# Stores of pairwise products from one DMA queue or from two: odd chunks issued from GpSimd, even chunks from SP

## The reference

```
_I, _J = np.triu_indices(NUM_FEAT, k=1)
proj = jnp.einsum('bnd,ed->bne', x, W)
out = proj[:, PAIR_I, :] * proj[:, PAIR_J, :]
```

## Time and profile before

| | |
|---|---|
| median of three runs | 511.1 us (510.85 to 511.14) |
| span of the profiled execution | 508.2 us |
| VectorE busy | 437.3 us, 86% |
| TensorE busy (matmul) | 71.3 us, 14% |
| ScalarE busy | 54.3 us, 11% |
| GpSimd busy | 0.7 us |
| bytes moved by DMA | 215.10 MB, 423 GB/s over the span |

### The profile page before, as it was taken

The page is one execution under the profiler, slowest core; times in us unless marked ns, Lnnn a source line. Parts: engine busy times, 40 slices in busy tenths (PEclk is TensorE's granted clock), DMA queues, the critical chain, the costliest instruction groups (busy, mean ns, idle before and its releaser), DMA issues.

```text
span 508.2 us, 2204 instructions
## 1 busy us (share of the span) xinstructions
PE 71.3 (14%) x481; PEld 65.4 (13%) x481; DVE 437.3 (86%) x220; ACT 54.3 (11%) x162; POOL 0.7 (0%) x6
## 2 busy tenths in 40 slices
PE   6965100000930000000660000000000000000000
PEld 5854100000920000000660000000000000000000
DVE  3999988888999999899999999999899989999900
ACT  5752000000720000000450000000000000000000
POOL 0000000000000000000000000000000000000000
PEclk9995555555875555555695555555555555555555
DMA  8999999999999999999999999999999999999996
GB/s 311 411 423 433 427 431 428 430 431 434 428 431 432 434 431 432 431 429 434 434 430 432 431 434 432 431 432 432 429 434 431 427 427 427 429 429 431 431 431 277
DMA packets 17430, 215.10 MB, mean 423 GB/s; under 512 B 1936, under 2 KB 2064, under 8 KB 7184
## 3 DMA queue, kind: packets, MB, share of 16 engines
q1 hardware_dynamic: 14400, 209.72, 96.7%
q10 hardware_dynamic: 3024, 5.31, 2.8%
HBM read 10.55 MB, written 204.47 MB: 423 GB/s over the span
## 4 chain that ended last, share of the span: by engine, by line
DMA 68%; DVE 21%; issue 5%; PE 1%; DVEq 0%; SPq 0%; ACT 0%; ACTq 0%
DMA out_dram<-products 67%; DVE products L248 21%; DMA w_in<-in_L_rec_W_dram 1%; PE proj_ps L182 0%; PE turned_ps L172 0%; SPq L145 0%; DVEq L248 0%; PE w_ps L162 0%; ACT proj L217 0%; ACT x_turned L206 0%; DVEq L271 0%; ACT w_turned L201 0%; SPq L144 0%; DVEq L247 0%; ACTq L205 0%
## 5 line engine op out<-in xcount | busy, mean ns | idle before, releaser
L248 DVE TENSOR_TENSOR products<-proj 128x384 f32 (+36 forms) x220 | 437.3, 2045 | 46.3 <-DMA out_dram<-products 37.3
L182 PE MATMUL proj_ps<-w_turned,x_turned 128*128 128x128 f32 x320 | 60.5, 319 | 181.5 <-ACT x_turned L206 181.3
L182 PEld LDWEIGHTS proj_ps<-w_turned,x_turned 128*128 128x128 f32 x320 | 48.9, 219 | 186.3 <-ACT x_turned L206 184.4
L206 ACT COPY x_turned<-turned_ps 128x256 f32<-128x256 f32 x80 | 30.0, 379 | 174.0 <-DVEq L257 171.9
L172 PE MATMUL turned_ps<-identity,x_in 128*128 128x128 f32 x160 | 34.4, 306 | 5.7 <-ACT proj L217 5.1
L217 ACT COPY proj<-proj_ps 128x256 f32<-128x256 f32 x80 | 29.7, 373 | 31.4 <-issue 19.0
L172 PEld LDWEIGHTS turned_ps<-identity,x_in 128*128 128x128 f32 x160 | 23.1, 161 | 6.6 <-issue 5.3
L201 ACT ACT_TABLE_LOAD x1 | 1.3, 1283 | 1.2 <-PEq L284 1.2
L162 PE MATMUL w_ps<-identity,w_in 128*128 128x128 f32 x1 | 0.4, 447 | 4.1 <-DMA w_in<-in_L_rec_W_dram 4.1
L162 PEld LDWEIGHTS w_ps<-identity,w_in 128*128 128x128 f32 x1 | 0.2, 182 | 4.0 <-issue 4.0
L201 ACT COPY w_turned<-w_ps 128x128 f32<-128x128 f32 x1 | 0.3, 265 | 2.1 <-PE w_ps L162 2.1
## 6 DMA issues: line engine op xcount, KB each, us to landing
out_dram<-products SPq DMA_DIRECT2D x80, 2496.0 KB, 24.0
x_in<-in_r_x_dram SPq DMA_DIRECT2D x20, 256.0 KB, 6.1
x_in<-in_r_x_dram ACTq DMA_DIRECT2D x20, 256.0 KB, 29.8
w_in<-in_L_rec_W_dram ACTq DMA_DIRECT2D x1, 64.0 KB, 3.2
```

The lines of the kernel that those rows point to most:

```text
L182: last = pe.matmul(proj_ps[group % 2][:, k, :], x_turned[group % 2][:, k, :], w_turned[:, :], start=True, stop=True)
L206: act.copy(x_turned[group % 2][:, :, :], turned_ps[group % 2][:, 0:GROUP, :]).then_inc(x_turned_ready, 1)
L248: last = dve.tensor_tensor(products[slot][:, place:place + count, :], proj[:, tile % 2, i:i + 1, :].broadcast_to([P, count, DIM]), proj[:, ...
```

## The change

The stores are divided by the parity of the chunk. SP keeps the even chunks, with its loop. GpSimd gets the odd chunks: after the identity matrix its program waits 40 times for `chunk_ready` and issues 40 stores, written out without a loop. Each buffer now has two semaphores, one for either queue. As five is odd, chunk c and chunk c - 5 in the same buffer have different parities, so VectorE waits for the other queue's semaphore each time, with the count of that queue's earlier stores from this buffer (`stored_before`). At the end SP waits for all ten semaphores.

```
-        stored = [sem(f"stored{s}") for s in range(SLOTS)]
+        stored_even = [sem(f"stored_even{s}") for s in range(SLOTS)]
+        stored_odd = [sem(f"stored_odd{s}") for s in range(SLOTS)]
...
             with sp.Fori(0, tiles) as tile:
-                for chunk in range(CHUNKS):
+                for chunk in range(0, CHUNKS, 2):
                     a, b = chunk_range(chunk)
                     sp.wait_ge(chunk_ready, tile * CHUNKS + (chunk + 1))
                     sp.nop(nofuse=True)
                     sp.dma_start(out[bass.ds(tile * P, P), a:b, :],
-                                 products[chunk % SLOTS][:, :, :]).then_inc(stored[chunk % SLOTS], 16)
+                                 products[chunk % SLOTS][:, :, :]).then_inc(stored_even[chunk % SLOTS], 16)
             for slot in range(SLOTS):
-                sp.wait_ge(stored[slot], 16 * tiles * ROUNDS)
+                sp.wait_ge(stored_even[slot], 16 * tiles * (ROUNDS // 2))
+                sp.wait_ge(stored_odd[slot], 16 * tiles * (ROUNDS // 2))
...
+            for tile in range(tiles):
+                for chunk in range(1, CHUNKS, 2):
+                    a, b = chunk_range(chunk)
+                    pool.wait_ge(chunk_ready, tile * CHUNKS + (chunk + 1))
+                    pool.dma_start(out[tile * P:(tile + 1) * P, a:b, :],
+                                   products[chunk % SLOTS][:, :, :]).then_inc(stored_odd[chunk % SLOTS], 16)
...
+            def stored_before(chunk):
+                kind = stored_odd if chunk % 2 == 0 else stored_even
+                same = [c for c in range(chunk % SLOTS, chunk, SLOTS) if c % 2 != chunk % 2]
+                return kind[chunk % SLOTS], 16 * len(same)
...
                 for chunk in range(CHUNKS):
-                    dve.wait_ge(stored[chunk % SLOTS], 16 * ROUNDS * tile + 16 * (chunk // SLOTS))
+                    stored, count = stored_before(chunk)
+                    dve.wait_ge(stored, 16 * (ROUNDS // 2) * tile + count)
                     multiply_chunk(tile, chunk)
```

More of the change, by code:

```diff
@@ L263, in _ @@
                 if chunk >= SLOTS:
-                    dve.wait_ge(stored[chunk % SLOTS], 16 * (chunk // SLOTS))
+                    stored, count = stored_before(chunk)
+                    dve.wait_ge(stored, count)
                 multiply_chunk(0, chunk)
```

## The result

The changed kernel takes 512.4 us as a median of seven runs (511.94 to 512.54), against 511.1 us (510.85 to 511.2, also seven): a ratio of 1.0026, 95% interval 1.0015 to 1.0036. That is small, 1.3 us, but the interval lies clear of 1, and the ratio lies over the 0.2% that the prediction took as its bound for no change (the lower end of the interval, 0.15%, does not): slower, where "nothing changes" was the forecast at 50% and slower had 33%. The range of 507.5 to 518 us holds it.

The account below looks back on a forecast made before the run. The prediction took the full DMA engines, at 431 GB/s, to bound the kernel. Its terms were all nothing: 508.2 + 0 + 0 + 0 = 508.2 us of span, 511.1 us as a median; range 507.5 to 518 us.

Parts of the forecast that it names:

- nothing changes: Likeliest case: whole-kernel time stays at 511.1 us, within 0.2% or about 1 us; chance 50%.
- slower: Three rivals together, 33%: engines slower with GpSimd's stores 25%, GpSimd holding up VectorE 6%, loads starving 2%.
- What bounds the kernel: DMA engines are full from 60 to 480 us (share 1.01, 431 GB/s); VectorE is paced by stores of 5.93 us.
- the sign of being right: From 60 to 480 us, the DMA engines would run at 430 to 432 GB/s.
- The issue on GpSimd: Each of GpSimd's 40 store issues takes 0.33 us, at most 5.75, hidden behind some 15 us of queued work; cost nothing.
- Two stores at once: Two queues share the engines, each store at half rate; landing takes 23.8 us against 23.7 with one queue; cost nothing.
- The rate: DMA engines stay at 431 GB/s with GpSimd's stores; cost nothing, with bounds of -3 and +22 us.
- My bound from below: GpSimd's half of the stores (237 us) at 391 GB/s, 9% less, would cost 22 us more.
- The loads: ScalarE's loads slow to 11.7 us each, at worst ten left at 20 us, last issued near 137 us; cost nothing.
- Waits and the end: VectorE's waits keep their places, SP waits for ten semaphores at the end, the tail stays 23.4 us; cost nothing.
- the four rivals: Engines slower with GpSimd's stores (25%), GpSimd holds up VectorE (6%), loads starve (2%), faster (17%).
- The base: Unchanged kernel: span 508.2 us, plus 2.9 us kept around it, giving the 511.1 us median.

Follow-up runs that it names:

- swapped: The changed kernel with the halves exchanged, GpSimd storing the even chunks and SP the odd ones: 510.9 us, ratio 0.9999.
- last_on_sp: The changed kernel with only the very last store (chunk 19 of tile 3) moved back to SP: 510.5 us, ratio 0.9990.

## Why the prediction was wrong

*What bounds the kernel: right.* The DMA share stays at 1.01, VectorE waits 37.2 us for stores after 37.3, its 4992-column product still takes 5.36 us, and all that was put beside other work stayed there. The long stretch at 429 GB/s lies a little under the 430 to 432 that were named as the sign of being right.

*The issue on GpSimd: the size off, the cover right.* 0.53 us in place of 0.33 us, on an idle engine. The longest was 0.67 us, so no issue was held up for the length of a product.

*Two stores at once: right.* 24.0 and 23.9 us to landing, 23.8 predicted.

*The rate: right for this kernel, at 0.3 us.* The last landing came at 508.1 us after 507.8. A slower rate was a real danger, though: with all 80 stores from GpSimd the last landing is 3.3 us late. (My bound from below was worked out wrong: 391 in place of 431 GB/s is 10% more time, so 24 us and not 22. Nothing hung on it.) The 429 GB/s of the long stretch would have misled: at the end of either kernel a chunk takes 5.93 us (and here the same):

```profile
462.67 5.43 DVE L230 TENSOR_TENSOR products<-proj 128x768 f32 x2 [0.50 <-DMA out_dram<-products]
468.60 5.43 DVE L230 TENSOR_TENSOR products<-proj 128x384 f32 x2 [0.50 <-DMA out_dram<-products]
```

*The loads: the cover right, the times not.* They are thinned out as said: ScalarE's queue was held for up to 23.6 us and, further on, 10.8 us (11.7 predicted), but only four loads were held, not ten, and the last was issued at 78.5 us, not 137. VectorE's waits for ScalarE went from 8.9 to 11.9 us. The stores in line covered that: VectorE's last product began at 480.7 us after 478.3, and the last store landed 0.3 us later.

```profile
L193 ACTq DMA_DIRECT2D x_in<-in_r_x_dram x20: 334/335/23592, 6.3 to 78.5; - x20
...
DMA to landing us min/median/max: 5.8/58.7/130.2
```

*Waits and the end: this step failed.* "It is issued with three others in line, and the tail remains at the 23.4 us for which SP waited; only an issue later than 15 us would show." I followed the tail to the last landing and stopped. What comes after it, the engines' meeting, was worth 0.2 us before; with 40 stores on GpSimd's queue and the last one among them it is 1.6 us. In the kernels whose GpSimd issues the last store the DRAIN ends 0.1, 0.9, 1.7 and 3.3 us behind GpSimd's last landing, for 1, 20, 40 and 80 stores, and `swapped` and `last_on_sp` take the loss away by ordering alone. Put into the sum, the closing barrier's 1.4 us more give 511.1 + 1.4 = 512.5 us; 512.4 was measured. None of the four rivals was this: a fixed piece behind the last byte was not among them.

*The base.* The 2.9 us around the span were 2.2 to 2.3 us in every later run of the kernel before; its profiled execution, at 508.2 us, was 0.5 us below the middle of its later spans (508.1 to 509.2). It did no harm here, since only the difference counted.

## What to carry to other kernels

Where the DMA engines are full, a second issuer moves no byte sooner; look instead at what it adds behind the last byte. A kernel ends when its slowest engine is through its closing instructions, not when the last store lands, so read the closing barrier's line and the wait of the first engine that reaches it. If GpSimd has to issue transfers, let another queue have the last ones: here the time from GpSimd's last landing to the end needs 0.041 us for each transfer of 2,496 KB that it issued; other sizes were not tried.

## What was not expected of the hardware

- The DRAIN's price grows with the number of transfers issued from GpSimd: 0.1, 0.9, 1.7, 1.7 and 3.3 us behind the last landing for 1, 20, 40, 40 and 80. The Trainium skill ("DMA: Bandwidth & Descriptors", "Issuing engines are not separate DMA queues") says that several issuers only save sequencer time; for the transfers themselves the traces agree (24.0 and 23.9 us), for the end of the program they add 1.4 us.
- Stores from GpSimd's queue alone slow the pace from 5.93 to 6.06 us, after a delay of 22 stores in one kernel and 46 in the other. The last three landings of both, all well behind GpSimd's last issue, come 5.93 to 5.97 us apart again. Between 420 and 480 us of the kernel with all 80, one store packet in twenty takes over 812 ns, where it is 761 ns in the kernel before; the medians are 749 and 747 ns. A few slow engines that first use up a lead over the others would give such a delay; that is argued, not shown, as no view here tells the engines apart, and it does not say why the pace comes back. The same page of the Trainium skill, in its table of measured facts, calls two of the 16 engines usually slower and guesses at the rings of GpSimd's descriptors; no run tested it.
- A slower pace is not bound to GpSimd alone, either: in the profiled execution of `last_on_sp`, the slowest of its eleven at 511.25 us, VectorE took 12.0 us for two chunks from 435 us on, where `swapped`, with the same two queues, took 11.9. Why is not shown.
- The queues fell into step in pairs. From 76 to 125 us VectorE of the changed kernel made two chunks without a wait between them and then waited 1.6 to 1.75 us, where before it waited about 1.1 us at nearly each. Over the whole run the waits for stores add up to the same, 37.2 us after 37.3.

```profile
76.54 10.77 DVE L230 TENSOR_TENSOR products<-proj 128x3584 f32<-128x3584 f32 x4 [1.59 <-DMA out_dram<-products]
89.03 10.77 DVE L230 TENSOR_TENSOR products<-proj 128x1920 f32<-128x1920 f32 x4 [1.72 <-DMA out_dram<-products]
```
